# A graph network kernel: identity matmuls added ahead of TensorE's waits

## What is computed

```python
x = _layernorm(x + L0(x))   # edge MLP: 64 -> 64 -> 128 -> 64 -> 32, mean over the edges of a node
x = _layernorm(x + L1(x))   # normalised sum of neighbours
x = _layernorm(x + L2(x))   # the same with a 32x32 weight, a bias and relu
x = _layernorm(x + L3(x))   # three GATv2 layers, each with 8 heads, self loops and a batch norm

def _gatv2(x, src, dst, Wl, Wr, att, bias):
    xl, xr = (x @ Wl).reshape(-1, 8, 32), (x @ Wr).reshape(-1, 8, 32)
    e = leaky_relu(xl[src] + xr[dst], 0.2)
    logits = einsum('ehc,hc->eh', e, att)
    alpha = softmax of logits over the edges of each dst
    return segment_sum(alpha[:, :, None] * xl[src], dst).mean(axis=1) + bias
```

## Time and profile before

| | |
|---|---|
| median of 3 runs | 6000.18 us (5997.96 to 6010.52) |
| profiled execution, one core | span 7770.9 us |
| mean granted clock of PE | 0.821 |
| busy, share of the span | PE 74%, DVE 46%, ACT 23%, POOL 52% |
| instructions | PE 43965, DVE 6811, ACT 3748, POOL 4236 |
| gathers (indirect DMAs on POOL) in the stages | 4220 |

### The profile page before, as it was taken

The page is one execution under the profiler, slowest core; times in us unless marked ns, Lnnn a source line. Parts: engine busy times, 40 slices in busy tenths (PEclk is TensorE's granted clock), DMA queues, the critical chain, the costliest instruction groups (busy, mean ns, idle before and its releaser), DMA issues.

```text
span 7770.9 us, 130521 instructions
## 1 busy us (share of the span) xinstructions
PE 5760.6 (74%) x43965; PEld 3691.2 (48%) x43965; DVE 3565.2 (46%) x6811; ACT 1748.7 (23%) x3748; POOL 4059.1 (52%) x4236
## 2 busy tenths in 40 slices
PE   5888886566646666578887876877787758788777
PEld 4666665455545454334444443444444424444444
DVE  5444444455544444444444444444444534444446
ACT  2222222344420000022222221222222122222221
POOL 4555554666646566455555533555555245555551
PEclk8888887777767776688888897888888878888988
DMA  4444443222212222233333332333333223333332
GB/s 103 129 129 129 128 128 98 51 56 56 56 47 56 55 56 55 49 82 93 88 91 88 89 85 56 90 90 89 92 89 89 80 58 92 89 89 93 91 88 65
DMA packets 688913, 648.23 MB, mean 83 GB/s; under 512 B 401396, under 2 KB 483771, under 8 KB 688251
## 3 DMA queue, kind: packets, MB, share of 16 engines
q1 hardware_dynamic: 548266, 463.96, 20.0%
q0 software_dynamic: 135616, 175.22, 11.8%
q10 hardware_dynamic: 4368, 0.70, 0.1%
HBM read 550.21 MB, written 89.17 MB: 82 GB/s over the span
## 4 chain that ended last, share of the span: by engine, by line
PE 43%; issue 22%; another core or an unknown queue 21%; DVE 9%; ACT 3%; DVEq 2%; DMA 0%; POOL 0%; ACTq 0%; POOLq 0%
PE ps L1055 14%; PE ps L900 7%; PE ps L994 5%; PE ps L1005 2%; PE ps L1015 2%; PE ps L855 2%; PE ps L915 1%; PE ps L980 1%; DVE region L1778 1%; DVE acc L1803 1%; PE ps L974 1%; PE ps L864 1%; ACT region L662 1%; PE ps L811 1%
## 5 line engine op out<-in xcount | busy, mean ns | idle before, releaser
L381 POOL DMA_INDIRECT rows<-table,idx x2340 | 2258.3, 965 | 2221.5 <-ACT region L651 1042.6
L1055 PE MATMUL ps<-region,hot 128*128 128x272 f32 x4992 | 1528.3, 457 | 295.8 <-DVE region L1756 159.4
L1055 PEld LDWEIGHTS ps<-region,hot 128*128 128x128 f32 x4992 | 1040.8, 219 | 690.9 <-issue 461.8
L1803 DVE TENSOR_TENSOR acc<-acc,ps 128x272 f32 x1248 | 544.5, 436 | 1685.6 <-remote 808.6
L662 ACT ACTIVATE region<-ps 128x512 f32<-128x512 f32 x1248 | 677.3, 595 | 2691.7 <-remote 1438.8
L900 PE MATMUL ps<-hot,region 128*128 128x192 bf16 (+1 forms) x6144 | 896.1, 309 | 444.2 <-issue 429.0
L900 PEld LDWEIGHTS ps<-hot,region 128*128 128x128 bf16 x6144 | 703.4, 123 | 590.9 <-issue 529.9
L368 POOL DMA_INDIRECT rows<-table,idx x728 | 696.6, 957 | 534.2 <-PE ps L835 320.4
L994 PE MATMUL ps<-xT,wcat 64*128 64x512 f32 x2496 | 771.8, 696 | 170.4 <-issue 92.1
L1778 DVE TENSOR_TENSOR region<-ps,region 128x1056 f32<-128x1056 f32 x582 | 724.7, 1251 | 44.0 <-issue 40.4
L398 POOL DMA_INDIRECT rows<-table,idx x576 | 546.6, 949 | 378.5 <-issue 157.3
(11 more groups left out here) (304 smaller groups left out, 6646.9 us busy)
## 6 DMA issues: line engine op xcount, KB each, us to landing
hot<-hot_dram SPq DMA_DIRECT2D x624, 256.0 KB
turned<-turned_dram SPq DMA_DIRECT2D x624, 128.0 KB
rows<-table,idx POOLq DMA_INDIRECT x3644
hot_dram<-hot SPq DMA_DIRECT2D x104, 512.0 KB
xwin<-table SPq DMA_DIRECT2D x1664, 24.0 KB
region<-hot_dram SPq DMA_DIRECT2D x64, 512.0 KB
region<-d_dram SPq DMA_DIRECT2D x104, 256.0 KB
turned_dram<-turned SPq DMA_DIRECT2D x104, 256.0 KB
```

The source lines that it names most:

```text
L381: pool.indirect_dma_start(rows[:, n % 2, j, :], None, table, bass.IndirectOffsetOnAxis(ap=idx[:, s:s + 1], axis=0)).then_inc(rows_in3[n % ...
L1055: mm = pe.matmul(ps[:, sum_bank(k, side, i), 0:PC + H], hot[:, b, 4 * side + 2 * i + j, :], px[b][:, 4 * side + 2 * i + j, :], start=(j == ...
L1803: v.tensor_tensor(at, at, ps[:, sum_bank(k, side, i), 0:PC + H], ALU.add).then_inc(att_added, 1)
```

## The change

Two helpers issue matmuls whose result is not read: the identity times the identity, repeated over 512 moving columns, into a whole bank, or over 448 columns into columns 64 to 511 of bank DEG, beside the degree counts. The first helper writes bank 0 (edge pass and attention), which the next `rows_in` writes over. The calls stand in the PE stream at fixed places and with fixed counts.

```diff
+        full_moving = identb[:, :].unsqueeze(1).broadcast_to([P, 4, P])
+        part_moving = identb[:, 0:112].unsqueeze(1).broadcast_to([P, 4, 112])
+        def keep_warm(pe, bank, times):
+            for _ in range(times):
+                pe.matmul(ps[:, bank, :], identb[:, :], full_moving, start=True, stop=True, skip_group_check=True)
+        def keep_warm_beside(pe, bank, times):
+            for _ in range(times):
+                pe.matmul(ps[:, bank, 64:512], identb[:, :], part_moving, start=False, stop=False, skip_group_check=True)
...
             for s in range(G + 2):
                 if 0 <= s - 1 < G:
                     first_layer(s - 1)
+                    keep_warm(pe, 0, 1)
                 if s + 2 < G:
                     read_one(s + 2)
...
                 if s < G:
+                    if s > 0:
+                        keep_warm(pe, 0, 2)
                     rows_in(s)
...
                 if kind == "dense":
                     read(i)
+                    keep_warm_beside(pe, DEG, 3)
                     if i > 0:
                         sum_dense(i - 1)
+                    keep_warm_beside(pe, DEG, 2)
...
                 if u < G:
                     z_half(u, 0)
+                    keep_warm(pe, XT, 1)
                 if phase == 1 and ends:
+                    if u < G:
+                        keep_warm(pe, XT, 4)
                     pe.wait_ge(carry_made, at + 1)
...
                 if phase == 2 and ends and done > 0:
+                    if u < G:
+                        keep_warm(pe, XT, 2)
                     pe.wait_ge(fdiag_made, at + 1)
...
                 if u + 1 < G:
+                    keep_warm(pe, XT, 2)
                     rows_in(u + 1)
```

## The result

The changed kernel takes 6137.53 us (6135.54 to 6139.48, 4 runs) against 5999.07 us for the one before: a ratio of 1.0245, 95% interval 1.022 to 1.0269. It is slower by 138 us where 40 us less were forecast. It lies 2.5 us inside the upper end of the stated range of 5790 to 6140, on the side of rival C.

A forecast was written before the change was run, and what follows sets the result against it. POOL's gathers were taken to set the pace nearly everywhere: 5275 + 621 + 48 = 5944 us, 56 under the median. Of those 56, 40 were given to steps at the low clock: 6000 - 40 = 5960 us, range 5790 to 6140.

The forecast's parts named there:

- rival C: Attention: PE becomes the pace, 9.87 us a step against 9.56: 6097 us; 0.28, shared with fillers not lifting the clock.
- The bound, from the gathers' sum: Whole kernel: 5275 us of gathers, 621 without gathers and 48 filling pipelines make 5944, 56 us under the measured median.
- Steps 2 and 3, the prices: PE: a filler costs 0.22 us (512 columns) or 0.19 (448) at high clock; a low-clock group loses 1.6 us.
- Steps 4 and 5, edge pass and convolutions: Edge pass: 8.6 us a step with fillers, under POOL's 8.75; convolutions: at most 534 against 720 a pass, change 0.
- Step 6: Attention: PE needs 8.2 us a step before and 9.0 with fillers, under POOL's 9.38.
- What would show it: Profile after: clock over 0.93, attention over 0.95; L1055 groups 2.0 to 2.1 us; gathers 1.25 us apart; longer span.
- The bound of 6020: Whole kernel: a time over 6020 us would show the prediction wrong and say PE had no room in attention.

The follow-up runs named there:

- the second profile: The kernel before, unchanged, profiled again because the first profile's execution spanned 7770.9 us: 5992.34 us, ratio 1.0004, span 5992.6 us.

## Why the prediction was wrong

**The bound, from the gathers' sum.** 4220 gathers at 1.25 us are 5275 us: right, in every kernel that was run. The remainder was put together wrongly. The 621 us without gathers came from the held-up execution; in the second profile they are 574. The 48 for filling the pipelines, read off the longest waits of that execution, are 29 in the edge pass and 3 and 1 in the convolutions. And POOL's waits for ACT L651 were put at nothing, as the recording's: the second profile still has 75.9 us of the 1042.6. So the room over the gathers was not 56 us but 144, of which 111 in attention (36, 39 and 36 us a layer), and the three layers were where something other than the gathers set the pace. A sum that closes to 1% on the measured time was taken for proof that its parts were right.

**Steps 2 and 3, the prices.** 0.22 us for a filler of 512 columns at the high clock: right, 0.23 measured. Groups at half speed cost 1.6 us: right as read from the earlier trace rows, but those rows were of the held-up execution, whose clock in attention was 0.86; in the second it is 0.97. Over the whole span the clock is 0.904 there, so 19% of it is at the low level and not 36%. The gain that the fillers were to bring in attention was nearly not there to be had, and the other stages show that a higher clock is worth at most 0.3% of the time there.

**Steps 4 and 5, edge pass and convolutions.** Right in time: the fillers fit under the gathers, with 6 to 9 us of gain and nothing. In clock they were half right: 0.96 in the edge pass, but 0.88 and 0.86 in the convolutions, where I had said over 0.93.

**Step 6, the step that failed.** The rows said 9.04 us of PE a step, and I took 8.2, because I put a good part of the handover between groups down to the recording. The second profile, in an execution as long as the timed ones, shows PE's groups at 73.0 / 8 = 9.1 us a step, L1055 in the same 2.03 to 2.10 us as in the earlier trace rows, and 0.6 us of waits for DVE on top: 9.7. The handover is real, and the waits for DVE were a term that I didn't have. The point from which rival C decides, 8.73, was passed by the rows as they stood. That they come so near to 9.1 is in part luck: the same product on the second profile, 913.72 x 0.97 / 104, is 8.5, since the first ten steps of a layer have no sums in them. The idle 2.67 us of the earlier trace rows, taken for a wait for DVE at a chunk's end, are no such wait either: at the same place of a step with u % 8 = 2, ahead of the first L1055, the second profile has none (4144.04 above); its wait for DVE comes later in the step, at 4150.83. With PE's need as it is, the mechanism of C came true: PE is the pace in attention, and a chunk went from 77.8 to 81.8 us. The fillers are 8 x (0.23 + 0.53) and about 1.5 at the chunk's end, 7.5 us a chunk; 2.4 us of that lie in waits that got shorter (19.1 us in 7.9 chunks after, 4.8 a chunk before), 3.9 are the loss, 39 x 3.9 = 152 us, and 1.2 are not accounted for. Rival C's price, 97 us with no cover, was too low since its need of 9.87 a step had no waits for DVE in it: a step takes 81.8 / 8 = 10.2. C compared its need with 9.56 for a step that took 9.7, a smaller error that goes the other way. Measured, the difference is 0.5 us a step where C had 0.31.

**What would show it.** The gathers' 1.25 us, the clock of the edge pass and of attention, and L1055's 2.0 to 2.1 us for a group (605 of its 624 groups are under 2.15) came as written. The span "longer than before in spite of it" didn't, since the first profile was an exception. The bound of 6020, over which PE had no room in attention, was the right signal.

## What to carry to other kernels

Work put in to keep an engine's clock up is free only inside a wait that is really waited out, and only as long as nothing else has shortened that wait; where the engine has nothing to wait for, it is added to the engine's path, and here that was 3 us a chunk. Ask first which engine paces the stage: in the convolutions the clock rose from 0.80 to 0.88 and the time stayed. Before using a profile that is much longer than the timed runs, take another one: stalls, clocks and sums over idle stretches of such an execution are its own, while the durations of single groups at the high clock carry over (L1055: 2.0 to 2.1 us in both). To find which of two nearly balanced engines paces a loop, take a little work from each in turn: 390 us off the gathers gave 43, and one small matmul issued 2 us earlier gave 83.

## What was not expected of the hardware

The recorded execution of the same program spanned 7770.9 us once and 5992.6 us another time, with PE's instructions about 0.7 us apart for stretches of 10 us only in the long one (L900 stood on "issue" 452 times there and once in the other); what brings that about was not tried. The clock in the convolutions rose from 0.80 only to 0.88 and 0.86 with 1280 fillers that took PE's busy share from 65% and 62% to 75% and 74%, and in attention it was 0.97 without any.
